# A cross-attention's output projection issued one sequence later, behind the next logits, and its addition behind the first row minimum

## What is computed

```
Q = layernorm(x) @ Wq.T + bq;  K = ctx @ Wk.T + bk;  V = ctx @ Wv.T + bv     # 16 heads of 8
D = clip(frac[k] - frac[q], -0.2, 0.2)
logits = gamma * Q K.T / sqrt(8) + delta * (alpha_pos * max(D, 0) + alpha_neg * min(D, 0))
out = softmax(logits) V
x = x + tanh(g_xattn) * (out @ Wo.T + bo)
```

## Time and profile before

| | us |
|---|---|
| median of 3 executions | 1914.29 (1913.93 to 1918.66) |
| the profiled execution, its own time | 1919.0 |
| its span, first to last instruction | 1916.2 |
| mean granted TensorE clock in the span | 0.981 |
| TensorE matmuls busy over the span | 1742.9 (91%) |
| DVE / ACT / POOL busy over the span | 1613.1 (84%) / 1389.4 (73%) / 1331.6 (69%) |
| opening of slot 2's first mask to that of slot 15 | 53.51 to 233.65 |

### The profile page before, as it was taken

The page is one execution under the profiler, slowest core; times in us unless marked ns, Lnnn a source line. Parts: engine busy times, 40 slices in busy tenths (PEclk is TensorE's granted clock), DMA queues, the critical chain, the costliest instruction groups (busy, mean ns, idle before and its releaser), DMA issues.

```text
span 1916.2 us, 85177 instructions
## 1 busy us (share of the span) xinstructions
PE 1742.9 (91%) x33584; PEld 1377.8 (72%) x33584; DVE 1613.1 (84%) x3868; ACT 1389.4 (73%) x3701; POOL 1331.6 (69%) x1226
## 2 busy tenths in 40 slices
PE   5888869999899999899998899998999998999997
PEld 3444447787777787777787777787787776787776
DVE  6666679999679999589998699996799995899985
ACT  4677657877677877577886677885777875777875
POOL 4444457888478888388887488885688874888882
PEclk9899879999999999999999999999999999999999
DMA  5000011111021111021111211111211110211111
GB/s 130 5 5 4 2 59 42 33 38 40 24 74 41 33 40 39 23 75 40 33 37 32 67 41 40 33 37 31 68 43 38 33 43 20 76 40 39 33 36 48
DMA packets 59087, 77.46 MB, mean 40 GB/s; under 512 B 16608, under 2 KB 31674, under 8 KB 57914
## 3 DMA queue, kind: packets, MB, share of 16 engines
q1 hardware_dynamic: 58938, 75.36, 15.1%
HBM read 22.63 MB, written 1.05 MB: 12 GB/s over the span
## 4 chain that ended last, share of the span: by engine, by line
PE 59%; DVE 14%; ACT 9%; POOL 8%; issue 8%; SPq 1%; DMA 0%; POOLq 0%; DVEq 0%; ACTq 0%
PE y_ps L524 9%; PE s_ps L476 7%; PE proj_ps L455 7%; PE tr_ps L465 6%; POOL qk L1519 5%; PE pv_ps L506 4%; PE proj_ps L457 4%; PE proj_ps L456 4%; ACT square L818 4%; DVE by_cos L1091 3%; PE s_ps L698 3%; DVE by_sin L1091 3%; DVE sumsq L1103 3%; PE y_ps L516 2%; PE proj_ps L684 2%
## 5 line engine op out<-in xcount | busy, mean ns | idle before, releaser
L1512 POOL TENSOR_TENSOR qk<-by_cos,by_sin 128x512 f32<-128x512 f32 x388 | 498.4, 1285 | 199.1 <-DVE by_sin L1091 198.0
L1519 POOL TENSOR_TENSOR qk<-qk,inv_norm 128x512 f32<-128x512 f32 x388 | 404.4, 1043 | 82.2 <-ACT inv_norm L824 67.9
L818 ACT ACTIVATE square<-proj_ps 128x512 f32<-128x512 f32 x364 | 217.6, 598 | 110.0 <-PE proj_ps L457 92.9
L455 PE MATMUL proj_ps<-w_hi,x_hi 128*128 128x512 f32 x546 | 268.2, 491 | 22.9 <-DVE by_sin L1091 20.3
L1091 DVE TENSOR_TENSOR by_cos<-proj_ps,tab 128x512 f32<-128x512 f32 x364 | 249.9, 687 | 34.4 <-ACT square L818 32.5
L465 PE MATMUL tr_ps<-ident,qk 128*128 128x128 f32 x1544 | 238.7, 277 | 40.2 <-POOL qk L1519 25.5
L1103 DVE TENSOR_REDUCE sumsq<-square 128x8 f32<-128x512 f32 x388 | 262.3, 676 | 0.0
L465 PEld LDWEIGHTS tr_ps<-ident,qk 128*128 128x128 f32 x1544 | 181.1, 142 | 110.3 <-POOL qk L1519 79.1
L1091 DVE TENSOR_TENSOR by_sin<-proj_ps,tab 128x512 f32<-128x512 f32 x364 | 247.8, 681 | 0.0
L1525 POOL TENSOR_TENSOR s_sb<-s_sb,row_max 128x512 f32<-128x512 f32 x192 | 205.0, 1068 | 32.5 <-DVE row_max L1122 31.7
L457 PE MATMUL proj_ps<-w_hi,x_lo 128*128 128x512 f32 x546 | 217.1, 398 | 0.0
(11 more groups left out here) (173 smaller groups left out, 4160.5 us busy)
## 6 DMA issues: line engine op xcount, KB each, us to landing
arena<-v SPq DMA_DIRECT2D x388, 130.0 KB, 2.4
w_raw<-in_L_ffn_Wqkv SPq DMA_DIRECT2D x7, 1536.0 KB, 6.8
wo<-in_L_ffn_Wo SPq DMA_DIRECT2D x7, 512.0 KB, 3.9
w_raw<-in_L_ffn_W SPq DMA_DIRECT2D x7, 341.0 KB, 6.2
c_in<-in_ctx SPq DMA_DIRECT2D x16, 64.0 KB, 1.8
xn<-in_fside_BxS SPq DMA_DIRECT2D x1, 1024.0 KB, 6.1
out<-z SPq DMA_DIRECT2D x4, 256.0 KB, 2.9
w<-in_L_ffn_W SPq DMA_DIRECT2D x12, 64.0 KB
```

The costliest lines, as they stand in the source:

```text
L455: pe.matmul(ps[:], x_hi[:], w_hi[:, col], start=True, stop=False)
L818: act.activation(square[:, c % 2, :], ps[QK_AT[c] % 2][:], ACT.Square).then_inc(squared, 1)
L1512: pool.tensor_tensor(heads(qk[:, c, :]), heads(by_cos[:, c % 2, :]), heads(by_sin[:, c % 2, :])[:, :, ::-1, :], ALU.add).then_inc(qk_added, 1)
L1519: pool.tensor_tensor(ap, ap, inv_norm[:, c, :].unsqueeze(2).to_broadcast([128, 8, DH]), ALU.mult).then_inc(qk_ready, 1)
```

## The change

On TensorE the output projection leaves the end of the slot. `x_out_project(T - 2)` is issued in slot T behind `x_scores(T, par, 0)`, that is behind both groups of the first logits and ahead of `x_p_transpose(T - 1, 2)`; slots 0 and 1 issue none. One call, for sequence 14, stands ahead of the tail behind slot 15, where the one at the end of slot 15 stood. On DVE `x_add(T - 2)` changes places with `x_minima(T, 0)`.

```
@@ tensor
-            def x_slot(T, par, first=False, front_on=True):
+            def x_slot(T, par, first=False, second=False, front_on=True):
                 x_scores(T, par, 0)
+                if not first and not second:
+                    x_out_project(T - 2)
                 if not first:
                     x_p_transpose(T - 1, 2)
...
                 x_values(T, par, 0)
-                if not first:
-                    x_out_project(T - 1)
...
-            x_slot(1, 1)
+            x_slot(1, 1, second=True)
...
+            x_out_project(NB - 2)
             x_p_transpose(NB - 1, 2)
@@ vector
                     x_sums_inverse(T - 1, 3)
+                x_minima(T, 0)
                 if not first and not second:
                     x_add(T - 2)
-                x_minima(T, 0)
```

## The result

The changed kernel takes **1894.19 us** (median of 4 runs, 1892.18 to 1897.38) against 1916.47 (4 runs, 1913.93 to 1918.81) on the same chip: a ratio of 0.9885 (95% interval 0.9871 to 0.9899), 22.3 us less. Its profiled execution took 1892.18, with a span of 1890.4; the execution read before took 1919.0, with a span of 1916.2.

A forecast was written before the change was run, and what follows sets the result against it. A loop of dependences through TensorE's end-of-slot projection wait was taken to bound the cross-attention. From 1919.0 us, 14.4 (11 x 1.17 + 2 x 0.74) for the wait and 8.0 for the clock gave 1897 us, range 1886 to 1909.

The forecast's parts named there:

- The loop of dependences: Cross-attention slots: scores, mask, reciprocal, POOL, transposes, second scores set the time; without the wait each boundary gains 1.17 us.
- The odd slots: Odd cross-attention slots at full clock, 13.12 us undisturbed, were to last 11.95 us.
- The gain there is 149.87 - 148.65 = 1.22 us: Logits at a slot's start come 1.22 us earlier: the wait and the projection's two matmuls.
- Slots 14 and 15: Boundaries into these slots gain only 0.74 us each, since POOL's weight subtraction ends 0.74 before its next multiplication.
- The clock: Of 12.0 us lost to TensorE's lower clock in thirteen slots, two thirds, 8.0 us, would go with the wait.
- The third that I kept for other causes: One third of the 12.0 us at lower clock stays, for falls such as behind DVE's casts before slot 2.
- The projection's new place: TensorE, ahead of the transposes: takes 0.25 us there, costing the loop nothing, covered by DVE's 0.76 us wait.
- The addition: On DVE behind the first minima: waits for nothing at full clock, up to 0.6 us at lower; costed at nothing.
- The clock stays: Rival: the wait's 14.4 us come but the clock's 12.0 us remain, 1904.6 us, or 1900 from the median; chance 0.33.
- ACT is the bound: Rival: TensorE's time is hidden behind ACT, nothing moves, 1914 to 1919 us; chance 0.13 together with the edit not acting.
- The projection becomes the wait: Rival: scores start no earlier and the projection delays transposes, 3.3 to 6.4 us slower, 1922 to 1925; chance 0.04.
- The change doesn't do what it says: Rival: TensorE stalls at the new place as at the old, time stays; chance 0.13 together with ACT as bound.

The follow-up runs named there:

- the twelve constants: Changed kernel plus twelve matmuls of constants behind slot 1 alone: 1890.71 us, 2.0 less than the unaltered changed kernel; slot 2 lasts 11.50 instead of 12.93.
- the filled kernel: Kernel before plus four matmuls of constants ahead of each projection in the slots, issued into its wait: 1906.89 us, ratio 0.9943 to the kernel before.
- VectorE's part alone: Kernel before with only the row minimum moved ahead of the addition, projection left at the end of the slot: 1916.81 us, ratio 1.000.
- The kernel with four projections: Changed kernel with the projection issued four times in its new place: 1895.01 us, ratio 0.9886 to the kernel before; slots of 11.98.
- the later place: Changed kernel with the projection one step later, ahead of the last group's transposes: 1893.93 us, ratio 0.9882 to the kernel before.
- the wait put back: Changed kernel with TensorE again waiting for the attention at the end of each slot, projection left in its new place: 1919.16 us, ratio 1.001 to the kernel before.

## Why the prediction was right, and where its steps were off

The forecast was 1897 us, the range 1886 to 1909; 1894.19 lies in it, and "faster" (under 1908.5) was right. The terms, slot by slot at full clock, give the account of the 27.7 us. One view of the kernel before is needed for it, TensorE from slot 9 into slot 10, over the loop's edge at full clock:
```profile
160.13 0.43 PE L591 MATMUL pv_ps<-p_T,arena 128*32 128x128 f32 x8
161.52 0.49 PE L599 MATMUL y_ps<-arena,x_att_T 128*128 128x128 f32 x2 [0.96 <-ACT x_att_T L897]
162.09 0.50 PE L558 MATMUL s_ps<-pos_hi,w_hi 128*128 128x512 f32 x1
```

- **The loop of dependences: right.** The mask follows the logits at 123.89 by 125.14 - 123.89 = 1.25 (1.24 was read before), the reciprocal is bounded by ACT's sums, DVE's idle time is 0.60 (0.65 forecast) and ACT's 0.39 (0.45 forecast). A slot of 12.77 became 11.58, 1.19 less against 1.17.
- **The odd slots: undersized.** They were to become 11.95 and became 11.58, 1.54 less than 13.12. Before, the projection waited at the loop's edge too, and the scores came 0.57 behind its start (162.09 - 161.52) where the earlier trace rows have 0.25; now L558 comes 0.36 behind L591 at the edge as inside. The step "The gain there is 149.87 - 148.65 = 1.22 us" was read inside a pass and carried over to the edge, where it is larger by 0.3. That is some 2 us of the total, for the five odd slots 3 to 11. Slot 13, behind which the loop ends, lasted 12.82 before at full clock and not 13.12.
- **Slots 14 and 15.** The subtraction between slots 13 and 14 shows in slot 14's length, 12.04, a gain of 0.73; into slot 14 the full gain came (12.82 - 11.56 = 1.26), so one of the two reductions to 0.74 was not needed in the thirteen slots. The other subtraction (206.18 to 208.56) lies behind slot 15's mask; whether it is part of the 1.2 us that the rest takes longer was not tried. Together the wait is worth 1.27 (slot 2, 12.77 - 11.50) + 5 x 1.54 + 1.26 + 5 x 1.19 + 0.73 = 16.9 us instead of 14.4.
- **The clock: undersized.** "I take two thirds, 8.0": with slot 13 at 12.82 the undisturbed lengths add up to 167.8, so 12.3 us and not 12.0 lay at the lower clock. Only slot 2's fall, 13.01 - 11.50 = 1.5, was left, so 10.8 went. 16.9 + 10.8 = 27.7. The third that I kept for other causes was too much: the one fall left is that in slot 2, behind DVE's casts, where the twelve constants show its cost. (In the kernel before, it does not come every time: the filled kernel and the one with VectorE's part alone have slot 2 at 1.00, 12.75 us.) That the waits made the falls was an argument from one row then; the filled kernel shows it.
- **The projection's new place: right at 0, for the wrong reason.** I named DVE's 0.76 wait as cover. The kernel with four projections shows a nearer limit, ACT emptying the transposes' bank, with 0.26 us to spare. Had the projection taken 0.6, the forecast would have called it free, and by these rows it would have cost some 0.1.
- **The addition: right.** It starts at 115.33, behind a projection that began at 114.17, and waits for nothing; moved back, it changes nothing.
- **The rivals.** "The clock stays" (1904.6) falls by the clock of 0.99. "ACT is the bound" falls: ACT, with 9.65 of 11.58 us, is still the engine with the most work that doesn't overlap, and taking a wait from TensorE gave 22.3 us. TensorE's weight loads are 6.20 of 11.58 us. By the rule of the Trainium skill (Perfetto Trace Analysis, Identifying the Most-Contended Engine), as the prediction read it, 1919 came out; the measured 1894.19 is against that reading. "The projection becomes the wait" falls by the scores, which start right behind the values, and by the later place, which gains nothing. "The change doesn't do what it says" falls by the projection's wait, which is gone from the thirteen slots.
- **From the profile to the medians.** The forecast started from an execution of 1919.0, 4.7 above the median then shown. Profiled executions differ by 26.8 us, medians by 22.3. With the two terms at their measured size the same sum gives 1919.0 - 27.7 = 1891.3, 2.9 under the median; so that 1897 came near the median is in part luck.

## What to carry to other kernels

In an engine that runs its instructions in order, look at what stands behind each wait: an instruction whose result nobody needs soon should not hold back one that opens the next round of the loop. Where the granted clock of TensorE falls in some passes of a loop and not in others, look for the wait ahead of the fall and either take it away or fill it with matmuls of constants into an idle bank: here the one shortened thirteen slots by 27.7 us, of which 10.8 are the clock's, the other by 12.4, with constants that just fit into the wait. And before calling a new place free, follow the operand *and* the buffer that come free behind it: the cover may be on another engine than the one you looked at.

## What was not expected of the hardware

- Matmuls that compute nothing pay. Four of them in each 0.96 us wait took 10.5 us from the kernel before; 48 in the waits that were left brought the changed kernel to 1884.39. The clock of slots 2 to 14 went from 0.90 to 1.00 with the first, that of the tail from 0.83 to 0.96 with those in the tail.
- A fall of the clock follows a wait of this size only sometimes: with the same 0.96 us, slots 8 and 9 ran at 1.00 and slot 10 at 0.88, and of the thirteen waits six were followed by a fall. A single slot at full clock is no proof that its waits are harmless.
- The loop's edge on TensorE shows only behind a wait: 0.57 against 0.25 us from the projection to the scores before, 0.56 against 0.23 in the filled kernel, whose projection still waits for its operand, 1.51 against 1.04 idle with the wait put back, and 0.36 at the edge as inside in the changed kernel, where no wait stands ahead of it.
